# First mixture part: z's two norms on GpSimd, an expert's rounding and low half in its own step

## The chip, the core and the metric

The program runs on one core of a Trainium2 chip. Its engines are TensorE (PE; its weight loads are listed apart as PEld), VectorE (DVE), ScalarE (ACT), GpSimd (POOL) and SyncE (SP), which issues the DMAs. Each engine works through its own list of instructions in order and meets the others only at semaphores. The metric is the time of one execution in microseconds (us).

## The reference, cut to what matters

```python
x = x + 0.5 * ffn(layernorm(x))     # mixture of 8 experts, the best 2 of each row, and a shared expert
x = x + attn(layernorm(x))          # 16 heads, then an MLP; each projection normalises its input again
x = x + 0.5 * ffn(layernorm(x))     # the same mixture once more

def ffn(x):
    scores = sigmoid(x @ gate_W) * route_scale
    topk_scores, topk_idx = top_k(scores, 2)
    gate_full = einsum(topk_scores / topk_scores.sum(-1), one_hot(topk_idx, 8))
    h = gelu(einsum('bsd,edh->bseh', x, W1) + b1)
    expert_out = einsum('bse,bsed->bsd', gate_full, einsum(h, W2) + b2)
    return expert_out + gelu(x @ Ws1 + bs1) @ Ws2 + bs2
```

x is 4096 rows of 256. What the attention reads is z = layernorm(x1) of the first mixture's result x1, normalised once more (zn = layernorm(z)) and transposed (zT).

## The kernel before

It runs four parts one after the other: the first mixture (tiles named f_...), attention (a_...), the MLP (m_...), the second mixture (g_...). The change is in the first mixture alone (`ffn_phase` with `tail` set). The second mixture runs the same function without `tail`: it has no z.

A mixture goes over 8 blocks of 512 rows, numbered 0 to 7, and each block over 9 steps, e = 0 to 8: step 0 is the shared expert, the others are the eight experts. Each float32 operand of a product is split in a rounded high half and a low half, and three products are made of them. For one step the work is:

- TensorE: the first layer fl(e), 6 matmuls of 512 columns into f_hid (L938), and then the second layer of two steps before, sl(e-2), 12 matmuls of 256 columns into f_acc (L980).
- ScalarE: the gelu of f_hid into f_act_out (L515), and hi, the rounding of a hidden tile into the high half of f_hp (L507).
- VectorE: the gating g(e) = gate times f_act_out into f_gated (L737), and lo, the low half of f_hp (L742). Both read two tiles of SBUF. (In blocks 0 and 1 the gate comes from PSUM; from block 2 on from f_gB.)

sl(e) waits for lo(e). What differs between the parts is where hi(e) and lo(e) stand: in the first mixture ScalarE makes hi(e-1) in step e, right after the gelu of e, and VectorE makes lo(e-1) in step e, right after g(e), ahead of the other work of the step. In the second mixture hi(e) stands in step e itself, where it waits for g(e), and lo(e) too: at once in steps 0, 3 and 8, and behind the step's other work in the others.

The other work of VectorE in block i, by step: 1 result(i-1) (L753); 2 the logits of i+1 (L666, L668) and z_stats, the statistics of f_res (L631, L636); 3 choices(i+1), the best two (L685 to L694); 4 gates(i+1), small operations (L701 to L720); 5 zz_stats, the statistics of f_zz; 6 x_stats(i+2) and gate_stack (L727); 7 x_norm(i+2) into f_xn (L652), which waits for GpSimd's x_rstd(i+2); 8 zt_lo (L784); 0 xt_lo (L659).

z of block i-1 goes through three engines during block i: z_stats on VectorE; z_rstds on GpSimd (L589, L590, L592, L602: minus mean, variance + eps, to the power -0.5, their product); z_norm on ScalarE in step 4 (L446, four operations of 128x256, f_zz from f_res); the statistics of f_zz on VectorE in step 5; z_rstds again; zn_norm on ScalarE in step 7 (L446, f_zn from f_zz); the transposes of f_zn on TensorE in step 8 (L905).

GpSimd's list for block i is: expneg(i+1) (L606, a power over 128x32, behind the logits and needed by choices), z_rstds twice, x_rstd(i+2) (L590, L592). The blocks 2 to 5 are two rounds of a loop with two blocks in it; blocks 0, 1, 6 and 7 are written out. Blocks 6 and 7 have no x_stats and no x_norm, block 7 no choices. z of block 7 is normalised inside the attention's first steps, on ScalarE.

Of the kernel before, what the change touches and what calls it, by code (L numbers as in the profile page):

```python
# [23 lines left out]
ALU = mybir.AluOpType  # L24
# [100 lines left out]
def ffn_phase(nc, turns, tag, src, dst, w, tail):  # L125
# [150 lines left out]
    def has(i, ahead=0):  # L276

        return not isinstance(i, int) or 0 <= i + ahead < NB
# [163 lines left out]
    def on_scalar(act):  # L442
# [6 lines left out]
        def z_norm(i):  # L449
            act.wait_ge(s["z_rstd"], i * 2 + 1)  # L450

            act.wait_ge(s["z_out"], i * 16 + 16)
            normalise(zz, res, zrs, zshift, s["z"])

# [54 lines left out]
        def body(i, par, first, last):  # L509
            for e in range(NE):  # L510
                act.wait_ge(s["hid"], i * NE + e + 1)
                if e >= 3 or not first:
# [3 lines left out]
                               bias=b1[:, weights_of(e):weights_of(e) + 1]).then_inc(s["gelu"], 1)  # L516
                if tail or first:
                    if e > 0:
                        hi(i, e - 1, first)
                    elif not first:  # L520
                        hi(i - 1, E, False)
                else:
                    if e == 0 and isinstance(i, int) and i == 1:
                        hi(0, E, False)
                    hi(i, e, first)
                if now("up_x", e, first) and not last:
                    xt_hi(i + 1, 1 - par, up_bank(i))
                if now("gf", e, first) and not last:
                    gate_copy(i + 1)
                if e == 4 and tail and not first:  # L530
                    z_norm(i - 1)
                if e == 7 and tail and not first:
                    zn_norm(i - 1)
                if e == 8 and tail and not first:
# [29 lines left out]
        over_blocks(act, body)  # L564
        if tail:
            hi(NB - 1, E, False)
        return dict(z_norm=lambda: z_norm(NB - 1), zn_norm=lambda: zn_norm(NB - 1),
                    zt_hi=lambda c, ps: zt_hi(NB - 1, c, ps))

    def on_gpsimd(pool):  # L570
# [13 lines left out]
        def rstds(stats, ready, rstd, veps, powed, n, minus_mean=None):  # L584
# [7 lines left out]
            pool.tensor_tensor(rstd[:], rstd[:], mhalf[:], ALU.pow).then_inc(powed, 1)  # L592

        def x_rstd(i):
            rstds(mv, s["stats"], rs, s["veps"], s["rstd"], i + 1)
# [13 lines left out]
        def body(i, par, first, last):  # L609
# [4 lines left out]
            if tail and not first:  # L614
                z_rstds(i - 1, 0)
                z_rstds(i - 1, 1)
            if has(i, 2):
                x_rstd(i + 2)
# [9 lines left out]
    def on_vector(dve):  # L628
# [198 lines left out]
        def body(i, par, first, last):  # L827
            for e in range(NE):
# [4 lines left out]
                if e == 1 and not first:  # L833

                    result(i - 1)
                behind = not (tail or first) and e not in (0, 3, NE - 1)
                if tail or first:
                    if e > 0 and not (tail and first and e == 1):
# [53 lines left out]
        over_blocks(dve, body)  # L892
        if tail:
            lo(NB - 1, E)
        result(NB - 1)
# [1389 lines left out]
```

## Time and profile before

| | us |
|---|---|
| median of 3 runs (2415.49 to 2415.98) | 2415.65 |
| the profiled execution | 2414.72 |
| its span in the profile | 2412.9 |
| first mixture, first layer of block 1 to the attention's first product (53.28 to 275.72) | 222.44 |
| the same stretch, TensorE busy | 215.90 |

The profile is of one execution. A line of the timeline is: start in us, duration in us, engine, line of the kernel, operation, tile written <- tiles read, shape, count, and in square brackets how long the engine had been idle before it and who released it. Neighbouring operations on one engine overlap by some 0.08 us, so that a row's end is a little behind the next row's start. The clock that TensorE was granted is 1.00 in every block of the stretch.

### The profile page before, as it was taken

What the parts mean: (1) busy time and instruction counts of PE and PEld (TensorE: products, weight loads), DVE (VectorE), ACT (ScalarE), POOL (GpSimd) and SP (SyncE); (2) the same over time, 40 slices, a digit from 0 to 9 for tenths busy, and PEclk for the clock granted to TensorE, in tenths of its full rate; (3) what the DMA queues carried; (4) which work ended last, traced back from release to release, by engine and by line L of the source; (5) the groups of instructions that cost most, each with busy time, mean ns of one, the idle gap of its engine ahead of it and who ended that gap; (6) DMA issues with size and microseconds to landing.
All of it is one profiled execution on the core that took longest, in us unless ns stands there. A gap on an engine that the chain in (4) does not pass through costs nothing.

```text
span 2412.9 us, 46345 instructions
## 1 busy us (share of the span) xinstructions
PE 2374.6 (98%) x14512; PEld 2068.2 (86%) x14512; DVE 1867.4 (77%) x3615; ACT 1684.6 (70%) x2932; POOL 1521.8 (63%) x1536
## 2 busy tenths in 40 slices
PE   8999999999999999999999999999999999999999
PEld 7888878888888888888888888888888889998898
DVE  7887687888878788887878878788887875466775
ACT  4555677877878787787878778787787865443444
POOL 1333368787777877778787777878777765542220
PEclk9999999999999999999999999999999999999999
DMA  4744631222212232221223312122221345431332
GB/s 181 264 165 156 211 114 45 96 80 78 96 44 87 61 96 75 64 96 44 87 62 97 102 36 96 44 87 84 82 96 44 110 165 166 137 116 58 130 125 95
DMA packets 131970, 245.67 MB, mean 102 GB/s; under 512 B 7290, under 2 KB 90132, under 8 KB 120052
## 3 DMA queue, kind: packets, MB, share of 16 engines
q1 hardware_dynamic: 131828, 244.15, 31.0%
q8 instruction: 44, 0.72, 0.1%
q14 instruction: 98, 0.80, 0.1%
HBM read 140.12 MB, written 53.67 MB: 80 GB/s over the span
## 4 chain that ended last, share of the span: by engine, by line
PE 83%; DVE 7%; issue 4%; POOL 3%; ACT 2%; DMA 2%; SPq 0%; DVEq 0%; POOLq 0%; ACTq 0%
PE a_ov L1727 20%; PE a_sc L1691 19%; PE a_tr L1703 19%; PE a_pj L1638 7%; PE a_pj L1645 4%; PE g_acc L980 3%; PE g_hid L938 3%; PE f_acc L980 2%; PE f_hid L938 2%; PE m_proj L2141 1%; POOL m_zin L1987 1%; PE m_hid L2210 1%; DMA f_xin<-in_x 1%; DVE f_hp L742 1%; DVE f_gated L737 1%
## 5 line engine op out<-in xcount | busy, mean ns | idle before, releaser
L1594 DVE TENSOR_REDUCE a_nmax<-a_sc 128x1 f32<-128x1024 f32 x512 | 626.8, 1224 | 252.1 <-PE a_sc L1691 248.3
L1437 ACT ACTIVATE a_pT<-a_tr 128x512 fp32r<-128x512 f32 x1024 | 559.6, 596 | 317.2 <-PE a_tr L1703 312.3
L1521 POOL TENSOR_SCALAR a_pr<-a_pr,a_rden 128x1024 f32<-128x1024 f32 x512 | 576.5, 1127 | 282.3 <-DVE a_rden L1599 212.1
L1605 DVE TENSOR_TENSOR a_pT<-a_tr,a_pT 128x512 fp32r<-128x512 f32 x1024 | 650.4, 677 | 17.1 <-ACT a_pT L1437 17.1
L1727 PE MATMUL a_ov<-a_pT,a_v_s 128*128 128x512 f32 x2032 | 594.1, 414 | 1.2 <-DVE f_zT L784 0.8
L1443 ACT ACTIVATE a_pr<-a_sc,a_nmax 128x1024 f32<-128x1024 f32 x512 | 573.7, 1121 | 20.2 <-DVE a_nmax L1594 17.9
L1691 PE MATMUL a_sc<-a_k_s,a_q_s 128*128 128x512 f32 x2048 | 556.6, 393 | 0.6 <-DMA a_k_s<-a_k_s 0.6
L1703 PEld LDWEIGHTS a_tr<-f_ident,a_pr 128*128 128x128 f32 x4096 | 476.0, 140 | 79.8 <-DVE a_pT L1605 7.3
L1703 PE MATMUL a_tr<-f_ident,a_pr 128*128 128x128 f32 x4096 | 537.1, 273 | 1.8 <-DVE a_pT L1605 1.7
L1691 PEld LDWEIGHTS a_sc<-a_k_s,a_q_s 128*128 128x128 f32 x2048 | 376.6, 188 | 76.7 <-DMA a_k_s<-a_k_s 0.8
L1727 PEld LDWEIGHTS a_ov<-a_pT,a_v_s 128*128 128x128 f32 x2032 | 343.8, 189 | 47.5 <-issue 4.8
L1638 PE MATMUL a_pj<-a_z_s,a_wqk_s 128*128 128x512 f32 x756 | 213.9, 392 | 1.5 <-ACT a_staged L1398 1.1
L1638 PEld LDWEIGHTS a_pj<-a_z_s,a_wqk_s 128*128 128x128 f32 x756 | 141.6, 188 | 33.7 <-ACT a_staged L1398 1.4
L980 PEld LDWEIGHTS f_acc<-f_w2p,f_hp 128*128 128x128 f32 x864 | 110.8, 190 | 19.5 <-DVE f_hp L742 14.6
L980 PE MATMUL f_acc<-f_w2p,f_hp 128*128 128x256 f32 x864 | 117.2, 285 | 7.4 <-DVE f_hp L742 7.1
L980 PEld LDWEIGHTS g_acc<-g_w2p,g_hp 128*128 128x128 f32 x864 | 111.9, 191 | 11.3 <-DVE g_hp L742 6.8
L980 PE MATMUL g_acc<-g_w2p,g_hp 128*128 128x256 f32 x864 | 115.7, 284 | 3.4 <-DVE g_hp L742 3.2
L1645 PEld LDWEIGHTS a_pj<-a_wv_s,a_z_s 128*128 128x128 f32 x756 | 105.8, 188 | 12.1 <-issue 0.7
L938 PE MATMUL f_hid<-f_xT,f_w1p 128*128 128x512 f32 x432 | 113.7, 398 | 0.0
L938 PE MATMUL g_hid<-g_xT,g_w1p 128*128 128x512 f32 x432 | 113.0, 397 | 0.0
L515 ACT ACTIVATE f_act_out<-f_hid,f_b 128x512 f32<-128x512 f32 x72 | 49.1, 684 | 91.0 <-PE f_hid L938 91.0
L1645 PE MATMUL a_pj<-a_wv_s,a_z_s 128*128 128x256 f32 x756 | 109.0, 280 | 0.3 <-ACT a_q_s L1405 0.3
(265 smaller groups left out, 3182.0 us busy)
## 6 DMA issues: line engine op xcount, KB each, us to landing
a_z_s<-zT SPq DMA_DIRECT2D x32, 1024.0 KB, 7.8
a_k_s<-a_k_s SPq DMA_DIRECT2D x62, 512.0 KB, 5.6
a_wqk_s<-w_split SPq DMA_DIRECT2D x64, 256.0 KB, 3.1
a_v_s<-a_v_b SPq DMA_DIRECT2D x16, 1024.0 KB, 4.6
att<-a_ao SPq DMA_DIRECT2D x32, 512.0 KB, 2.9
m_in<-att SPq DMA_DIRECT2D x16, 1024.0 KB, 5.9
f_gB<-f_gate_rows SPq DMA_DIRECT2D x12, 1024.0 KB, 4.9
g_gB<-g_gate_rows SPq DMA_DIRECT2D x12, 1024.0 KB, 4.7
```

What stands on the lines that cost most here:

```text
L938: o = pe.matmul(hid[:, (par + e) % 2], w1p[:, a, (c * NE + x) * HID:(c * NE + x + 1) * HID], xT[:, par, c, b], start=(n == 0), stop=(n == 5))
L980: o = pe.matmul(acc[:, t], hp[:, e % 3, a, t * P:(t + 1) * P], w2p[:, b, x * D:(x + 1) * D], start=False, stop=(e == NE - 1 and (a, b) == ...
L1437: act.activation(pT[:, (u // 4) % 2, 0, 4 * part:4 * part + 4, (u % 4) * P:(u % 4 + 1) * P], tr[:, part].rearrange("p (t q) -> p t q", t=4 ...
L1443: act.activation(pr[:, k % NP], sc[:, k % 2], ACT.Exp, bias=nmax[:, k % NP:k % NP + 1], accum_out=den[:, k % NP:k % NP + 1]).then_inc(s["e ...
L1521: pool.tensor_scalar(pr[:, k % NP], pr[:, k % NP], rden[:, k % NP:k % NP + 1], 1.0, ALU.mult, ALU.mult).then_inc(s["normed"], 1)
L1594: dve.tensor_reduce(nmax[:, k % NP:k % NP + 1], sc[:, k % 2], AX.X, ALU.max, negate=True).then_inc(s["negmax"], 1)
L1605: dve.tensor_tensor(to[:, 1], tr[:, part].rearrange("p (t q) -> p t q", t=4), to[:, 0].bitcast(F32), ALU.subtract).then_inc(s["tr_lo"], 1)
L1638: o = pe.matmul(bank[:], wqk_s[:, "QK".index(kind), h, a], z_s[:, h * 2 + b, part], start=(h == 0 and i == 0), stop=(h == 1 and i == 2), s ...
L1645: o = pe.matmul(bank[:, h * 2 * P:(h + 1) * 2 * P], z_s[:, c * 2 + a, part // 2, col:col + P], wv_s[:, c, b], start=(i == 0), stop=(i == 5))
L1691: o = pe.matmul(sc[:, k % 2, kb * BT:(kb + 1) * BT], q_s[:, slot, head, tile * P:(tile + 1) * P], k_s[:, slot, head, a, kb * BT:(kb + 1) * ...
L1703: o = pe.transpose(tr[:, part, j * P:(j + 1) * P], pr[:, (k - LAG) % NP, (4 * part + j) * P:(4 * part + j + 1) * P], ident[:])
L1727: o = pe.matmul(values_bank(v, last)[:], v_s[:, vslot, kt, 2 * vhead:2 * vhead + 2] .rearrange("p k f -> p (k f)"), pT[:, blk % 2, a, kt], ...
```

## The change

GpSimd gets a `normalise` of its own, a `tensor_scalar` with multiply and add and the two per-row numbers as operands, four of 128x256. z_norm and zn_norm of blocks 0 to 6 leave ScalarE's steps 4 and 7 for GpSimd's list: the first right behind the first z_rstds, the second right behind the second, ahead of x_rstd(i+2). z of block 7 stays on ScalarE. In blocks 1 to 7 of the first mixture, hi and lo stand in the expert's own step, as in the second mixture.

```diff
@@ on_scalar
-                if tail or first:
+                if first:
                     if e > 0:
                         hi(i, e - 1, first)
...
-                if e == 4 and tail and not first:
-                    z_norm(i - 1)
-                if e == 7 and tail and not first:
-                    zn_norm(i - 1)
...
-        if tail:
-            hi(NB - 1, E, False)
@@ on_gpsimd
+        def normalise(to, x, ready, n, counted):
+            pool.wait_ge(ready, n)
+            stand_alone(pool, turns)
+            for t in range(NT):
+                o = pool.tensor_scalar(to[:, t], x[:, t], zrs[:, t:t + 1], zshift[:, t:t + 1], ALU.mult, ALU.add)
+            o.then_inc(counted, 1)
...
             if tail and not first:
                 z_rstds(i - 1, 0)
+                pool.wait_ge(s["z_out"], i * 16)
+                normalise(zz, res, s["z_rstd"], i * 2 - 1, s["z"])
                 z_rstds(i - 1, 1)
+                if not (isinstance(i, int) and i == 1):
+                    pool.wait_ge(s["zT_ps"], i * DC - DC)
+                normalise(zn, zz, s["z_rstd"], i * 2, s["zn"])
             if has(i, 2):
                 x_rstd(i + 2)
@@ on_vector
-                behind = not (tail or first) and e not in (0, 3, NE - 1)
-                if tail or first:
+                behind = not first and e not in (0, 3, NE - 1)
+                if first:
...
-        if tail:
-            lo(NB - 1, E)
```

GpSimd in a block of the loop, from the second z_rstds on. Before:

```order
L589 TENSOR_SCALAR f_zshift<-f_zmv 128x4
L590 TENSOR_SCALAR f_zrs<-f_zmv 128x4
L592 TENSOR_TENSOR f_zrs<-f_zrs,f_mhalf 128x4
L602 TENSOR_TENSOR f_zshift<-f_zshift,f_zrs 128x4
L586 REGISTER_ALU
L590 TENSOR_SCALAR f_rs<-f_mv 128x4
L592 TENSOR_TENSOR f_rs<-f_rs,f_mhalf 128x4
```

and now (the line numbers of the changed kernel differ a little; L593 is its normalise):

```order
L584 TENSOR_SCALAR f_zshift<-f_zmv 128x4
L585 TENSOR_SCALAR f_zrs<-f_zmv 128x4
L587 TENSOR_TENSOR f_zrs<-f_zrs,f_mhalf 128x4
L604 TENSOR_TENSOR f_zshift<-f_zshift,f_zrs 128x4
L622 REGISTER_ALU
L593 TENSOR_SCALAR f_zn<-f_zz,f_zrs,f_zshift 128x256 x4
L581 REGISTER_ALU
L585 TENSOR_SCALAR f_rs<-f_mv 128x4
L587 TENSOR_TENSOR f_rs<-f_rs,f_mhalf 128x4
```

Four operations of 128x256 now stand between the second z_rstds and x_rstd (f_rs).

VectorE in a block of the loop, from gate_stack in step 6 to x_norm in step 7 and the gating of step 8. Before:

```order
L727 CAST f_gst<-f_gbc 128x512
L730 REGISTER_ALU
L737 TENSOR_TENSOR f_gated<-f_gB,f_act_out 128x512
L742 TENSOR_TENSOR f_hp<-f_gated,f_hp 128x512
L650 REGISTER_ALU
L652 TENSOR_SCALAR f_xn<-f_xin,f_mv,f_rs 128x256 x4
L730 REGISTER_ALU
L737 TENSOR_TENSOR f_gated<-f_gB,f_act_out 128x512
```

and now:

```order
L734 CAST f_gst<-f_gbc 128x512
L749 TENSOR_TENSOR f_hp<-f_gated,f_hp 128x512
L737 REGISTER_ALU
L744 TENSOR_TENSOR f_gated<-f_gB,f_act_out 128x512
L657 REGISTER_ALU
L659 TENSOR_SCALAR f_xn<-f_xin,f_mv,f_rs 128x256 x4
L749 TENSOR_TENSOR f_hp<-f_gated,f_hp 128x512
L737 REGISTER_ALU
L744 TENSOR_TENSOR f_gated<-f_gB,f_act_out 128x512
```

lo(6) has moved ahead of g(7), and lo(7) from behind g(8) to between x_norm and g(8).

## Rows read from the trace of the kernel before

**Rows 1.** Page, part 1: TensorE's busy us, share of the span, instructions

```profile
PE 2374.6 (98%) x14512; PEld 2068.2 (86%) x14512; DVE 1867.4 (77%) x3615; ACT 1684.6 (70%) x2932; POOL 1521.8 (63%) x1536
```

**Rows 2.** Waits of TensorE, 0 to 282 us: total, times, longest

```profile
PE f_acc L980 <- DVE f_hp L742: 7.1, 16, 1.0
```

**Rows 3.** Windows of blocks 3, 6, 7: length, busy time by engine

```profile
core 0: us, PE busy (x) PEld busy (x) DVE busy (x) ACT busy (x) POOL busy (x), PEclk, DMA share, GB/s
...
117.87:149.51 31.64, 30.59 (x205) 27.24 (x204) 25.45 (x86) 17.34 (x32) 11.50 (x11) 1.00 0.49 168
212.38:242.96 30.58, 30.22 (x205) 27.34 (x204) 23.03 (x74) 17.33 (x32) 9.87 (x9) 1.00 0.47 156
242.96:275.72 32.76, 31.13 (x202) 27.38 (x201) 24.66 (x46) 23.58 (x37) 6.63 (x8) 1.00 0.76 273
```

**Rows 4.** Timeline of TensorE, block 3: start, duration, what, idle before

```profile
137.10 1.70 PE L980 MATMUL f_acc<-f_w2p,f_hp 128*128 128x256 f32 x12 [0.39 <-DVE f_hp L742]
140.54 1.69 PE L980 MATMUL f_acc<-f_w2p,f_hp 128*128 128x256 f32 x12 [0.35 <-DVE f_hp L742]
147.19 1.69 PE L980 MATMUL f_acc<-f_w2p,f_hp 128*128 128x256 f32 x12 [0.32 <-DVE f_hp L742]
150.98 1.60 PE L980 MATMUL f_acc<-f_w2p,f_hp 128*128 128x256 f32 x12
```

**Rows 5.** Timeline of VectorE, block 3

```profile
131.83 0.69 DVE L737 TENSOR_TENSOR f_gated<-f_gB,f_act_out 128x512 f32<-128x512 f32 x1 [0.15 <-ACT f_act_out L515]
135.76 0.69 DVE L737 TENSOR_TENSOR f_gated<-f_gB,f_act_out 128x512 f32<-128x512 f32 x1 [0.55 <-DVE f_idx L694]
145.85 0.68 DVE L737 TENSOR_TENSOR f_gated<-f_gB,f_act_out 128x512 f32<-128x512 f32 x1
146.45 0.69 DVE L742 TENSOR_TENSOR f_hp<-f_gated,f_hp 128x512 fp32r<-128x512 f32 x1
147.56 1.38 DVE L652 TENSOR_SCALAR f_xn<-f_xin,f_mv,f_rs 128x256 f32<-128x256 f32 x4 [0.42 <-POOL f_rs L592]
```

**Rows 6.** Timeline of GpSimd and ScalarE, block 3

```profile
142.53 0.44 POOL L589 TENSOR_SCALAR f_zshift<-f_zmv 128x4 f32<-128x4 f32 x1 [7.66 <-DVE f_zmv L636]
144.80 0.20 POOL L602 TENSOR_TENSOR f_zshift<-f_zshift,f_zrs 128x4 f32<-128x4 f32 x1
145.20 2.06 ACT L446 ACTIVATE f_zn<-f_zz,f_zshift,f_zrs 128x256 f32<-128x256 f32 x4
145.87 1.56 POOL L592 TENSOR_TENSOR f_rs<-f_rs,f_mhalf 128x4 f32<-128x4 f32 x1
```

**Rows 7.** Groups: count, busy us, mean ns; last, L592's min/median/max ns

```profile
L1474 POOL TENSOR_SCALAR a_v_b<-a_staged 128x256 fp32r<-128x256 f32 x64 | 25.9, 405 | 0.0
L2022 POOL TENSOR_SCALAR m_w_in<-m_w_in,m_ln 128x512 f32<-128x512 f32 x2 | 1.4, 728 | 0.0
L507 ACT ACTIVATE f_hp<-f_gated 128x512 fp32r<-128x512 f32 x64 | 39.8, 622 | 0.0
...
L592 POOL TENSOR_TENSOR f_rs<-f_rs,f_mhalf x8: 1037/1562/1589, 7.2 to 208.7; 128x4 f32<-128x4 f32 x8
```

**Rows 8.** Timelines, VectorE beside GpSimd; last, L1569's min/median/max ns

```profile
69.04 0.68 DVE L742 TENSOR_TENSOR f_hp<-f_gated,f_hp 128x512 fp32r<-128x512 f32 x1
69.08 0.78 POOL L590 TENSOR_SCALAR f_zrs<-f_zmv 128x4 f32<-128x4 f32 x1
...
2142.05 3.28 POOL L1987 TENSOR_TENSOR m_xin<-m_xin,m_b 128x256 f32<-128x256 f32 x4 [2.02 <-DMA m_xin<-x]
2143.79 0.95 DVE L2076 TENSOR_TENSOR m_hid_s<-m_act_out,m_hid_s 128x512 fp32r<-128x512 f32 x1 [0.80 <-ACT m_hid_s L1941]
...
L1569 DVE TENSOR_TENSOR a_q_s<-a_staged,a_q_s x4: 684/687/1003, 282.6 to 285.0; 64x512 fp32r<-64x512 f32 x4
```

**Rows 9.** Timeline of TensorE, end of block 7

```profile
270.58 1.06 PE L905 MATMUL f_aux<-f_ident,f_zn 128*128 128x128 f32 x8 [0.15 <-ACT f_zn L446]
272.39 3.49 PE L980 MATMUL f_acc<-f_w2p,f_hp 128*128 128x256 f32 x24 [0.75 <-DVE f_hp L742]
```

More of the change, by code:

```diff
@@ L452, in z_norm @@
             act.wait_ge(s["z_out"], i * 16 + 16)
+            act.wait_ge(s["zn"], i)
             normalise(zz, res, zrs, zshift, s["z"])
```

## The prediction

> **What bounds the kernel now.** I read the page's busy shares first: TensorE is busy 98% of the span [rows 1], so the change can only give back waits of TensorE, or make new ones. Next its waits up to 282 us: second layers (L980) wait 7.1 us for VectorE's low halves, 16 times [rows 2]. The windows say where: block 3 takes 31.64 us, block 6, which has one such wait and no x_stats and x_norm, 30.58 [rows 3]. Block 3 has three, of 0.39, 0.35 and 0.32 us [rows 4]. Two waits more for 1.06 us more: one costs about 0.53, a third of it in matmuls that restart without a preloaded weight. So a steady block (2 to 5) can win at most 3 x 0.53 = 1.6 us, and with blocks 1, 6 and 7 the whole change at most some 10 us.
>
> Who makes the three waits? VectorE from g(3) at 131.83 to the end of lo(6), 146.45 + 0.69 = 147.14, when sl(6) starts at 147.19 [rows 4, 5]. In these 15.3 us it has almost no idle time (the 0.55 behind the choice of the best two is the largest [rows 5]). The low halves are late because they stand behind choices, gates, zz_stats and x_stats: VectorE's work in steps 3 to 6 is long, not ScalarE's. Before step 3 and in steps 8 to 2 it waits for others and catches up. A second chain lies beside it: VectorE's zz_stats, GpSimd's second z_rstds (142.53 to 145.00), x_rstd (its power ends at 145.87 + 1.56 = 147.43), x_norm on VectorE at 147.56, which had already waited 0.42 us for it [rows 5, 6]. What hangs on x_norm is free now: sl(7) starts at 150.98 with no wait [rows 4].
>
> **The change part by part, in a block of the loop.**
>
> 1. *ScalarE is relieved.* Two norms of four operations at 0.52 us (2.06 / 4 [rows 6]) go away, 4.1 us a block. ScalarE is busy 17.3 us of 31.64 [rows 3], and nobody waits for it in steps 3 to 7. Worth 0.
>
> 2. *lo in its own step.* From g(3) to lo(6) the new order has two VectorE operations fewer, lo(2) (now ahead of g(3)) and g(7) (now behind lo(6)). One takes 0.60 us to the next one's start (145.85 to 146.45 [rows 5]): -1.20. In step 3 lo follows its gating at once, so VectorE stands still while ScalarE rounds: 0.62 [rows 7] and some 0.1 of handovers, +0.75. The other roundings of the chain hide behind the step's other work (1.4 us and more). Sum -0.45 us a block in blocks 2 to 6: -2.2.
>
> 3. *The norms on GpSimd, their price.* No row has this form. Bounds: 0.41 us for 128x256 with constant operands (L1474) and 0.73 for 128x512 with one per-row operand (L2022) [rows 7]. I take 0.47, nearer to the row of the same size; four are 1.9 us, which is no more than ScalarE's 2.06. So f_zz comes no later than before, and zz_stats, which stands two steps' work behind it, is not delayed: choices and gates hide the first norm.
>
> 4. *The two engines hold each other up.* In the trace, a GpSimd operation of 128x4 that starts beside L742 takes 0.78 us, where another of 128x4 takes 0.20 [rows 6, 8]: it waits until L742 is through. The other way round: L2076, a subtraction of two SBUF tiles as L742 is, takes 0.95 us inside GpSimd's L1987 instead of 0.68, and L1569 took 1.00 once instead of 0.69 [rows 8]. So a gating or a low half that meets a running norm waits for the rest of one of its four operations, 0 to 0.47 us, and the norm then waits for VectorE's whole pair. On the chain to lo(6) two meetings are likely, one near g(4), one at lo(6), which moved forward to just where the second norm runs: +0.3 us a block in blocks 2 to 6, +1.5. (The Trainium skill, SBUF — State Buffer, section "Who interferes with whom", has the rule behind it: a VectorE instruction with two SBUF inputs contends with a GpSimd instruction that reads SBUF, and the one that comes second is blocked for the whole of the other. By that rule the trace agrees; if it did not hold, this item would be 0 and item 5 smaller.)
>
> 5. *x_rstd stands behind the second norm.* This is the term that decides. z_rstds ends at 145.00 [rows 6]. The second norm takes 1.9 us, held up by the pair lo(6), g(7) for 1.2, with handovers until 148.2. Then x_rstd, 1.4 to 1.5 us (some 0.3 us by my estimate for the sum with eps, and 1.04, the least of L592 [rows 7], for the power, since VectorE now stands still and does not disturb it): x_norm can start at 149.8 instead of 147.56. It takes 1.32, and lo(7), now behind it, 0.68: done at 151.8. sl(7), at 150.98 before and at about 150.8 by items 2 and 4, waits 1.0 us. Without item 4's blocking x_rstd would end 1.2 earlier and lo(7) at about 150.6, just in time: 0 to 1.0, and I take 0.95, since the meeting is nearly certain. Blocks 2 to 5: +3.8.
>
> 6. *What comes after lo(7).* g(8), then lo(8) at once behind its rounding (0.75), zt_lo, lo(0), xt_lo, for which the logits on TensorE wait: with lo(7) late and sl(7) started by it, five operations of 0.60 and two waits stand against two second layers, two first layers and the transposes. The sum is within 0.3 us of even; +0.25 in blocks 2 to 5: +1.0.
>
> 7. *The ends.* Block 1 has its gates in PSUM, so g does not meet the norm; x_norm did not wait there. +0.2. At the end of block 7 TensorE waits 0.15 us for zn and 0.75 for the last low half [rows 9], which both come earlier now: -0.8. What a longer first mixture costs later is nothing: attention takes over where it ends.
>
> Sum: -2.2 + 1.5 + 3.8 + 1.0 + 0.2 - 0.8 = +3.5 us. The profiled execution took 2414.72 us, so 2418.2; the median of the runs lies 0.93 above it, so 2419.2 for the median, +0.15%.
>
> **The rivals.**
>
> - *Slower by more, the norms are dear.* The price of one is up to 0.6 us (the 128x512 of L2022 less its longer row, plus a second per-row operand), and VectorE's small operations of gates, which also read two tiles, meet the first norm: each of four norm operations can hold VectorE once, up to 2 us on the chain to lo(6). Then a steady block loses 1 to 1.5 us more than in my sum: +8 to +13 us, 2424 to 2429. It decides from 0.55 us an operation on. For it: the bound row is an estimate's distance away. Against: in the first norm's time VectorE mostly does the choices, whose search reads little.
> - *Hidden.* The blocking is rare or short, x_rstd comes in time. Then item 2 stays (-2.2), item 4 and 6 fall to 0, item 5 to 0 or +1, the end gives -0.8: -2 to -3, 2412 to 2414. For it: the two engines met in blocks 2 to 6 before too, and none of the f_gated and f_hp rows of block 3 is longer than 0.69 [rows 5].
> - *The waits go.* The low halves are ready a step earlier for sl(3), whose wait stood behind the choices, and the 0.55 us of idle time behind the search [rows 5] goes with the order; with no blocking the block drops towards block 6's 30.58 [rows 3]: 5 x 1.0 + 0.8, so -5 to -9, 2407 to 2411. Against: the sum of VectorE's work to lo(6) hardly shrinks.
> - *Nothing moves*: gains and waits cancel, or VectorE's chain stays as it is; within the bound of no change.
>
> **How the numbers follow.** My sum with its own spread, 0 to +8 us (item 5 between 0.5 and 1.5, item 4 between 0.1 and 0.6): 0.50. Dear norms: 0.15. Hidden: 0.20. The waits go: 0.13. Nothing moves: 0.02. A measurement of this kernel tells 0.2% from no change, 4.8 us: 2410.8 to 2420.5 counts as the same. Of my own case 0.30 lies within and 0.20 above. Faster 0.13, same 0.52 (0.30 + 0.20 + 0.02), slower 0.35 (0.20 + 0.15). The range leaves out the upper end of dear norms and most of the last gain: 2412 to 2427.
>
> **What the changed profile would show.** GpSimd's norm rows: 0.45 to 0.5 us each when undisturbed, with some of 1 us and more in which VectorE's pair ran. x_norm (f_xn) with an idle time of 1.5 to 2.5 us before it, released by GpSimd, instead of 0.42. TensorE with a new wait at the first second layer of a block, sl(7), of about 1 us, and perhaps a small one at the logits; the waits at sl(3) gone, at sl(4) and sl(6) still there. f_gated and f_hp rows over 0.8 us in steps 4 and 6 to 7. ScalarE idle before each rounding, as in the second mixture. No f_gated or f_hp row longer than 0.7 would show item 4 wrong; x_norm at its old distance from zz_stats would show item 5 wrong; and if item 5 is wrong, so is the sign of the whole.

## The result, and the profile after

The changed kernel takes 2429.60 us in the median of four runs (2429.05 to 2432.94), the kernel before 2415.57 (2415.01 to 2415.98): a ratio of 1.0058, with a 95% interval of 1.0046 to 1.0070. That is 14 us slower. The sign that the sum gave is right, the size is not: 2419.2 was predicted, with 2427 as the upper end.

Nearly all of the loss lies in the first mixture: its blocks 1 to 7 take 13.9 us more, and the spans of the two profiled executions differ by 14.3 (2427.2 and 2412.9). The windows of the changed kernel by block, 1 to 7, each from one first layer of step 0 to the next; the columns are those of [rows 3]:

```profile
53.01:85.41 32.40, 31.95 (x214) 28.97 (x212) 26.67 (x85) 13.00 (x21) 15.02 (x19) 1.00 0.43 151
85.41:121.35 35.94, 32.42 (x205) 28.86 (x204) 27.84 (x90) 14.14 (x24) 15.92 (x19) 0.95 0.79 305
121.35:152.73 31.38, 30.55 (x206) 27.36 (x204) 23.33 (x78) 13.92 (x23) 16.01 (x19) 1.00 0.44 161
152.73:185.49 32.76, 31.08 (x205) 27.33 (x203) 25.55 (x84) 13.88 (x23) 16.28 (x20) 1.00 0.45 160
185.49:219.98 34.49, 32.58 (x206) 28.69 (x204) 25.75 (x84) 13.87 (x23) 16.37 (x20) 0.95 0.43 149
219.98:255.39 35.41, 32.60 (x206) 28.62 (x204) 25.98 (x79) 14.65 (x25) 16.47 (x18) 0.95 0.41 148
255.39:289.39 34.00, 30.18 (x201) 27.33 (x200) 24.36 (x45) 19.60 (x28) 14.67 (x16) 1.00 0.75 260
```

The third column from the right is the granted clock. It was 1.00 in every block before; now it is 0.95 in blocks 2, 5 and 6. Against the same windows of the kernel before:

| block | before, us | after, us | difference | made up of |
|---|---|---|---|---|
| 1 | 32.54 | 32.40 | -0.1 | |
| 2 | 32.05 | 35.94 | +3.9 | late transfer of f_xin 2.2, clock 1.7 |
| 3 | 31.64 | 31.38 | -0.3 | no wait at its first second layer, block 2 being late |
| 4 | 31.45 | 32.76 | +1.3 | waits |
| 5 | 31.42 | 34.49 | +3.1 | waits 1.4, clock 1.7 |
| 6 | 30.58 | 35.41 | +4.8 | waits 3.1 (1.05 at sl(7), 0.35 at the logits, 1.6 for f_zn), clock 1.7 |
| 7 | 32.76 | 34.00 | +1.2 | waits for f_zz and f_zn |
| sum | 222.44 | 236.38 | +13.9 | clock 5.1, transfer 2.2, the rest waits |

A fall of the clock is priced from two blocks of one kernel with nearly the same waits: block 5 less block 4 here is 34.49 - 32.76 = 1.7 us, and three pairs in the experiments give 1.7 to 1.8 as well. Where a block had a fall, the column gives it 1.7 us and the wait the rest; that is a way to share out the difference and not a measurement of each part.

**A steady block without the clock.** TensorE in block 4, the rows that answer to [rows 4]:

```profile
155.25 1.70 PE L985 MATMUL f_acc<-f_w2p,f_hp 128*128 128x256 f32 x12 [0.88 <-DVE f_hp L749]
...
159.04 1.60 PE L985 MATMUL f_acc<-f_w2p,f_hp 128*128 128x256 f32 x12
160.72 1.95 PE L920 MATMUL f_gbc<-f_gwp,f_xT 128*128 128x16 f32 x16
...
182.81 1.70 PE L985 MATMUL f_acc<-f_w2p,f_hp 128*128 128x256 f32 x12 [0.30 <-DVE f_hp L749]
```

The wait at sl(3) is gone, those at sl(4) (0.25 us, not shown) and sl(6) stay, and sl(7) at 155.25 waits 0.88 us. The logits at 160.72 start 1.68 us behind the start of sl(8) where 1.44 is normal, and take 1.95 instead of 1.85: the row has no wait in brackets, but against the usual start they are 0.24 us late.

The cause of the late sl(7) is on GpSimd and VectorE (the first group of rows is GpSimd's, the second VectorE's); they answer to [rows 5, 6]:

```profile
181.42 3.10 POOL L593 TENSOR_SCALAR f_zn<-f_zz,f_zrs,f_zshift 128x256 f32<-128x256 f32 x4 [0.21 <-POOL f_zshift L604]
...
184.81 1.04 POOL L587 TENSOR_TENSOR f_rs<-f_rs,f_mhalf 128x4 f32<-128x4 f32 x1
```

```profile
182.07 0.69 DVE L749 TENSOR_TENSOR f_hp<-f_gated,f_hp 128x512 fp32r<-128x512 f32 x1
182.68 0.88 DVE L744 TENSOR_TENSOR f_gated<-f_gB,f_act_out 128x512 f32<-128x512 f32 x1
...
185.98 1.38 DVE L659 TENSOR_SCALAR f_xn<-f_xin,f_mv,f_rs 128x256 f32<-128x256 f32 x4 [2.42 <-POOL f_rs L587]
187.27 0.69 DVE L749 TENSOR_TENSOR f_hp<-f_gated,f_hp 128x512 fp32r<-128x512 f32 x1
```

x_norm had waited 0.42 us for f_rs; now 2.42. Behind it stands lo(7) at 187.27, for which sl(7) at 188.02 had waited 0.90.

**What one norm costs.** All 28 operations of each of the two norms (duration in ns: least, median, largest):

```profile
L593 POOL TENSOR_SCALAR f_zz<-f_res,f_zrs,f_zshift x28: 548/556/2549, 70.8 to 275.5; 128x256 f32<-128x256 f32 x28
L593 POOL TENSOR_SCALAR f_zn<-f_zz,f_zrs,f_zshift x28: 549/556/1590, 81.3 to 284.5; 128x256 f32<-128x256 f32 x28
```

0.556 us, not 0.47. (The Trainium skill, GPSIMD Engine Reference, section "Elementwise — side-by-side cycle accounting", gives 2.6 cycles an element for an operation with two tensor inputs; an estimate from it, at the page's 1.2 GHz, is 0.555 us for 256 elements. The trace has that number, 0.556, for an operation with one tensor input and two per-row operands, a form which the section does not name. The section "Engine selection" of the same page calls one-input operations roughly line-rate, and for this form, one input and two per-row operands at 0.556 us, the trace disagrees.)

**The clock.** Two windows of 2 us behind block 5's logits, same columns (in the ones before and behind them the clock is 1.00), and TensorE's rows there:

```profile
196.00:198.00 2.00, 2.00 (x8) 1.66 (x8) 0.16 (x1) 0.48 (x1) 1.76 (x1) 0.54 0.41 80
198.00:200.00 2.00, 2.00 (x13) 2.00 (x13) 1.77 (x5) 0.84 (x2) 2.00 (x1) 0.61 1.08 380
```

```profile
193.49 1.95 PE L920 MATMUL f_gbc<-f_gwp,f_xT 128*128 128x16 f32 x16
195.29 2.19 PE L943 MATMUL f_hid<-f_xT,f_w1p 128*128 128x512 f32 x6
197.28 1.05 PE L977 MATMUL f_acc<-f_b2s,f_gst 128*128 128x256 f32 x4
```

From about 196 to 199.5 the granted clock was 0.50, the lower of the two levels (1.2 instead of 2.4 GHz), while TensorE was busy all the time: six products of 512 columns took 2.19 us instead of 1.63, and the four of L977 1.05 instead of 0.64. Nothing is marked as waiting in these rows. A reader who counts waits alone misses 1.7 us.

**Block 2.** SP's rows of before, then of after. The first is two loads of gates into f_gB with a wait between them, the second the first store of the split weights, the last the load of f_xin:

```profile
81.12 4.57 SPq L375 DMA_DIRECT2D f_gB<-f_gate_rows  x2
85.73 0.43 SPq L326 DMA_DIRECT2D w_kept<-f_w1p  x1
...
95.59 7.62 SPq L403 DMA_DIRECT2D f_xin<-in_x  x1
```

```profile
82.73 5.43 SPq L375 DMA_DIRECT2D f_gB<-f_gate_rows  x2
88.21 0.43 SPq L326 DMA_DIRECT2D w_kept<-f_w1p  x1
...
96.05 9.67 SPq L403 DMA_DIRECT2D f_xin<-in_x  x1
```

VectorE at the end of block 1, g(8) in before, then x_norm and g(8) in after:

```profile
84.64 0.69 DVE L737 TENSOR_TENSOR f_gated<-f_gbc,f_act_out 128x512 f32<-128x512 f32 x1
```

```profile
85.23 1.38 DVE L659 TENSOR_SCALAR f_xn<-f_xin,f_mv,f_rs 128x256 f32<-128x256 f32 x4 [1.73 <-POOL f_rs L587]
...
87.13 0.68 DVE L744 TENSOR_TENSOR f_gated<-f_gbc,f_act_out 128x512 f32<-128x512 f32 x1
```

and, in after, x_stats on VectorE and sl(6) on TensorE:

```profile
114.31 1.40 DVE L638 BATCH_NORM_STATS2 f_st<-f_xin 128x6 f32<-128x256 f32 x4 [2.49 <-DMA f_xin<-in_x]
```

```profile
117.48 2.81 PE L985 MATMUL f_acc<-f_w2p,f_hp 128*128 128x256 f32 x12 [2.88 <-DVE f_hp L749]
```

Why the load is late is read from these rows and from the kernel. The second of the two loads into f_gB waits for the semaphore `gated`, that is for g(8) of block 1 (`sp.wait_ge(s["gated"], used)`), and the 5 MB of split weights stand behind it in SP's list. g(8) starts at 87.13 instead of 84.64: x_norm of block 1 waits 1.73 us for f_rs, where it waited for nothing before, and lo(7), 0.60, now stands ahead of g(8). So the stores start 2.5 us later, at 88.21. In each of the eight kernels in which x_stats waits for this load, it ends that wait 25.6 to 26.1 us behind the start of the stores: 111.77 in before, 114.31 here. It is item 5 of the prediction once more, x_rstd behind the second norm, in a block where TensorE does not feel it and SP does. The copy of the gates to f_gf is 1.6 us late too (80.65 instead of 79.03, behind the rounding of step 6), but it has time: in norms_only (below) it is on time, g(8) starts at 86.87, and the load lands at 113.83 all the same. x_stats waits only 0.73 us for it there, since it comes later itself.

### The profile page after: what moved, and what is told of

The parts are those of the page before. It is cut to its first block, busy times and chain, and to the rows that moved or that the text cites. A ratio compares the mean times of both kernels' runs of the same rounds, so it can differ in the third digit from the quotient of the medians.

```text
span 2427.2 us, 46362 instructions
## 1 busy us (share of the span) xinstructions
PE 2381.7 (98%) x14512; PEld 2074.7 (85%) x14512; DVE 1869.1 (77%) x3615; ACT 1662.8 (69%) x2876; POOL 1556.3 (64%) x1592
## 4 chain that ended last, share of the span: by engine, by line
PE 78%; DVE 3%; issue 3%; POOL 2%; ACT 1%; DMA 1%; DVEq 0%; SPq 0%; POOLq 0%; ACTq 0%
PE a_ov L1732 19%; PE a_sc L1696 19%; PE a_tr L1708 18%; PE a_pj L1643 7%; PE a_pj L1650 4%; PE g_acc L985 3%; PE g_hid L943 3%; PE m_proj L2146 1%; POOL m_zin L1992 1%; PE m_hid L2215 1%; PE m_acc L2186 0%; POOL m_xin L1992 0%; PE g_gbc L920 0%; DMA m_xin<-x 0%; DVE g_gated L744 0%
## 5 line engine op out<-in xcount | busy, mean ns | idle before, releaser
L508 ACT ACTIVATE f_hp<-f_gated 128x512 fp32r<-128x512 f32 x64 | 40.4, 631 | 94.8 <-DVE f_gated L744 94.8
```

## The experiments

Thirteen kernels; a steady block is block 4 where nothing else is said (31.45 us before, 32.76 after). The ratio behind each time is that to the kernel before, with its 95% interval.

**own_step_only and norms_only: each half alone.**

```diff
 own_step_only, against the kernel before
-                if tail or first:        # ScalarE: hi(e - 1) in step e
+                if first:
-                behind = not (tail or first) and e not in (0, 3, NE - 1)
+                behind = not first and e not in (0, 3, NE - 1)
 norms_only: the changed kernel with these lines as before
```

> The kernel before with hi and lo in the expert's own step; both norms stay on ScalarE. Theory A (the norms on GpSimd are the whole cost, by holding x_norm and the transposes of f_zn up, and TensorE's lower clock follows from those waits): nothing late at sl(7), x_stats of block 2 waits for its DMA at most 0.5 us, clock 1.00 in every block; by items 2 and 7 of the prediction 2411 to 2416 us, at most 2416. Theory B (the order of hi and lo is the cost, since VectorE stands still for each rounding in step 3 and ScalarE's work is late): 2422 us or more, with the waits at sl(4), sl(6) and the clock drops kept. If the late gate row of block 1 comes from the order and not from the norms, block 2 alone keeps a wait for f_xin of some 2 us here (+2 to +4).

> The changed kernel with hi and lo back at the places of before (hi(e-1) and lo(e-1) in step e); both norms stay on GpSimd. Theory A: most of the loss stays, since x_rstd still stands behind the second norm and f_zn is still late in blocks 6 and 7: 2424 to 2432 us, a wait of TensorE for f_zn in blocks 6 and 7. lo(6) is a step later here, so the second norm meets other work: the wait at the second layer moves to sl(6) or sl(7) and is 0.5 to 1.5 us. Theory B: the loss goes with the order: 2414 to 2418 us.

Measured: own_step_only 2426.87 us, 1.0047 (1.0030 to 1.0064); norms_only 2425.44 us, 1.0040 (1.0026 to 1.0054). Both theories fall: either half alone costs 10 to 12 us, and both together not 22 but 14. No block of either has a granted clock under 1.00. The steady block of each, own_step_only first:

```profile
155.20:188.43 33.23, 30.79 (x205) 27.27 (x204) 25.81 (x85) 18.02 (x31) 11.12 (x11) 1.00 0.44 158
```

```profile
153.18:186.73 33.55, 30.88 (x206) 27.18 (x204) 26.17 (x84) 13.63 (x24) 17.19 (x19) 1.00 0.45 157
```

33.2 and 33.6 us: each is worse in a steady block than the whole change (32.8). In own_step_only the cause is a new wait, once in each of blocks 1 to 7; ScalarE's two rows show why:

```profile
187.61 1.07 PE L901 MATMUL f_aux<-f_ident,f_zn 128*128 128x128 f32 x8 [1.64 <-ACT f_zn L446]
```

```profile
184.86 0.63 ACT L507 ACTIVATE f_hp<-f_gated 128x512 fp32r<-128x512 f32 x1 [1.67 <-DVE f_gated L735]
185.40 2.07 ACT L446 ACTIVATE f_zn<-f_zz,f_zshift,f_zrs 128x256 f32<-128x256 f32 x4
```

hi(7), now in its own step, waits for g(7) and holds zn_norm behind it. So the two halves of the change need each other: the own step makes ScalarE a bad place for the norm where it stands. In norms_only x_norm waits 2.42 us as in the whole change, and lo(6) and lo(7) stand a step later, so that sl(7) waits 1.05, sl(4) 0.94 and sl(6) 0.53.

**x_first: x_rstd(i+2) ahead of the second norm.**

```diff
                 z_rstds(i - 1, 1)
+                if has(i, 2):
+                    x_rstd(i + 2)
...
                 normalise(zn, zz, s["z_rstd"], i * 2, s["zn"])
-            if has(i, 2):
-                x_rstd(i + 2)
```

> The changed kernel with x_rstd(i+2) ahead of the second norm in GpSimd's list. Item 5 of the prediction (x_rstd behind the norm makes x_norm, lo(7) and sl(7) late): the wait of x_norm for f_rs falls from 2.4 us to 0.5, the 0.9 us at sl(7) go in blocks 2 to 5, which is worth 3 to 4 us, and with them two of the three clock drops (another 3 us): 2422 to 2425 us. Against it: f_zn comes some 1.5 us later, and its transposes in step 8, which wait 0.16 to 0.24 us in blocks 2 to 5 now, wait 1 us and more there; if that is the tighter place, the wait only moves and the time is 2428 to 2432.

Measured: 2425.13 us, 1.0039 (1.0024 to 1.0053). The wait at sl(7) is gone and another stands a step ahead of it; the first row is the transposes of f_zn, the second sl(7), 1.47 us behind its first layer, without a wait, and the last the logits, which are in time:

```profile
153.98 1.07 PE L912 MATMUL f_aux<-f_ident,f_zn 128*128 128x128 f32 x8 [1.56 <-POOL f_zn L593]
...
156.27 1.60 PE L987 MATMUL f_acc<-f_w2p,f_hp 128*128 128x256 f32 x12
...
161.40 1.84 PE L922 MATMUL f_gbc<-f_gwp,f_xT 128*128 128x16 f32 x16
```

Its steady block, 32.7 us, is that of the changed kernel. GpSimd has the second norm and x_rstd to do between z_rstds and the end of the block, 4.5 us of work (3.10 and 1.35), and something waits for whichever is second. The time came out near the range expected, but not for the reason expected: a steady block won nothing. Blocks 5 and 6, in which the clock now stays at 1.00, take 1.8 and 3.3 us less than in the changed kernel; block 1 takes 2.7 us more (35.06), with a wait of 2.1 us for f_zn and a fall of the clock behind it, and block 7 1.3 more, with a fall too.

**keep_late and keep_early: the 5 MB of split weights elsewhere in SP's list.**

```diff
         body(1, 1)
-        if tail:
-            keep_weights()
 keep_late: behind body(NB - 2, 0) and store_qkv(2); keep_early: behind body(0, 0)
```

> The changed kernel with the three stores of the split weights (2304, 512 and 2304 KB) behind block 6 in SP's list, not behind block 1. Theory C (block 2's 3.9 us are a transfer: the stores start 2.5 us later and the load of f_xin lands late among them, x_stats waits 2.5 us, TensorE waits 2.9 us and its clock drops): block 2 falls from 35.94 to 31.8 to 32.4 us, no drop there, 2425 to 2427 us; blocks 5 and 6 keep theirs, unless the stores meet block 6. If the wait of x_stats was GpSimd's and not the transfer's, block 2 stays at 35 us and more and the time at 2429.

> The changed kernel with the three stores of the split weights ahead of the first store_qkv, behind block 0 in SP's list. With the stores behind block 6 the wait of x_stats for f_xin in block 2 went, but the time was lost at the start of attention, where TensorE waited 8.3 us for zT behind them. Theory C: block 2's wait of 2.9 us at sl(6) goes and nothing new comes if block 1 has room for 5 MB: 2426 to 2428 us. If the stores are in the way in block 1 instead (its gate rows and f_xres, or the load of f_xin for block 3), the wait moves there and the time is 2429 to 2433.

Measured: keep_late 2440.44 us, 1.0102 (1.0086 to 1.0119), of which a wait of 8.3 us for zT at the start of attention, behind the stores; keep_early 2431.63 us, 1.0071 (1.0054 to 1.0088). In both, x_stats of block 2 waits for no transfer and sl(6) only 0.32 us, so that part of theory C holds. But block 2 fell only to 33.9 us in both, since the waits of a steady block and a fall of the clock came in their place, and in blocks 3 to 6 the clock fell three times in each instead of twice. The whole time did not show what the edit cured, the block did. Net, little was to be had here: blocks 2 and 3 of keep_early take 65.0 us together without their two falls, at 1.7 each, those of the changed kernel 65.6 without its one, since block 2's lateness had spared block 3 its wait at sl(7). Where no such wait follows, in best (below), the transfer's absence is worth 1.4 us.

**warm: work for TensorE in the wait at sl(7).**

```diff
+                if tail and e == 0 and (par == 1 and not isinstance(i, int) or isinstance(i, int) and i == NB - 2):
+                    pe.wait_ge(s["gst"], i + 1)
+                    pe.wait_ge(s["gf"], i - 1)
+                    for t in range(6):
+                        pe.transpose(gbc[:, t % 2, 0:P], ident[:], ident[:])
                 if e >= 2:
...
                     second_layer(i - 1, E - 1 + e, 1 - par, False)
```

> The changed kernel with six transposes of the identity into an unused place of f_gbc on TensorE ahead of sl(7) in the first step of blocks 3, 5 and 6. They add work to the 0.9 us in which TensorE waits there for lo(7), and take no wait away. Theory D (the lower clock of blocks 5 and 6 follows from that idle time a few us earlier): no granted clock under 0.95 near 196 and 230 us, the two blocks shorter by 1.6 us each, 2426 to 2427 us. Rival: the clock falls for another reason (all the waits together, or the small matmuls of the logits), the two drops stay, 2429 to 2431 us.

Measured: 2429.32 us, 1.0060 (1.0043 to 1.0076), as the changed kernel. The transposes stand in blocks 3, 5 and 6. In block 6 the idle time at sl(7) fell from 0.90 to 0.23 us, and the clock fell all the same, at 232 us; it fell in block 3 too, which had no wait there. In block 5 it stayed, but so it did in block 5 of keep_early, with a wait of 0.88. Theory D has this against it. Nor does it explain norms_only, where sl(7) waits 1.05 us and the clock stays:

```profile
155.86 1.70 PE L989 MATMUL f_acc<-f_w2p,f_hp 128*128 128x256 f32 x12 [1.05 <-DVE f_hp L751]
...
161.08 1.85 PE L924 MATMUL f_gbc<-f_gwp,f_xT 128*128 128x16 f32 x16
```

What it has and the changed kernel lacks is logits that start at once: 161.08 is 1.42 us behind the start of sl(8). This led to theory F: late logits, and not the wait at sl(7), bring the lower clock.

**xt_first and late_logits: the logits in time in one kernel, late in the other.**

```diff
 xt_first, against the changed kernel, step 0 of blocks 1 to 6
+                        xt_hi(i + 1, 1 - par, up_bank(i))      # ScalarE
                     hi(i, e, first)
+                        xt_lo(i + 1, 1 - par, up_bank(i))      # VectorE
                         lo(i, e)
 late_logits, against the kernel before
+                            for t in range(NT):
+                                o = dve.bn_stats(st6[:, t], w2p[:, 0, t * 352:(t + 1) * 352].bitcast(F32))
+                            o.then_inc(s["late"], 1)
+                            dve.wait_ge(s["late"], i)
                         xt_lo(i + 1, 1 - par, up_bank(i))
```

> The changed kernel with the high and low halves of f_xT ahead of hi(0) and lo(0) in step 0 of blocks 1 to 6. Seen so far: the clock fell only 2.5 to 3.7 us behind logits that had themselves waited 0.24 us for the low half of f_xT (in the changed kernel, keep_late, keep_early and warm, though not behind each of them), and never behind logits that did not wait, also not in norms_only, whose sl(7) waits 1.05 us shortly before. Theory F (the late logits, not the wait at sl(7), bring the lower clock): the waits of 0.9 us at sl(7) stay, the logits start 1.43 us behind the start of sl(8), the drops of blocks 5 and 6 go; 2 x 1.6 us and 4 to 5 x 0.35: 2424 to 2426 us. Rival (theory D, the wait at sl(7) brings it): drops stay, 2427 to 2429.

> The kernel before with four statistics more on VectorE (of 128x352 each, of a constant tile, into a scratch tile, unused) ahead of the low half of f_xT in step 0 of blocks 1 to 6, so that the logits wait 0.2 to 0.4 us and nothing else on TensorE does. Theory F: two to five of the six blocks show a granted clock of 0.50 for some 3.4 us a few us behind the logits, at 1.6 us each, and with 6 x 0.35 for the waits 2420 to 2426 us. Theory D: no drop, since nothing waits at sl(7); only the waits are paid: 2416.5 to 2418 us.

Measured: xt_first 2426.01 us, 1.0039 (1.0024 to 1.0054); late_logits 2423.36 us, 1.0030 (1.0018 to 1.0041). Block 5 of xt_first and TensorE in it; then blocks 3 and 5 of late_logits, and TensorE in block 3 (the logits start 1.68 us behind sl(8)):

```profile
186.41:219.03 32.62, 30.80 (x206) 27.27 (x203) 25.74 (x84) 13.76 (x23) 16.79 (x20) 1.00 0.46 169
```

```profile
188.93 1.70 PE L989 MATMUL f_acc<-f_w2p,f_hp 128*128 128x256 f32 x12 [0.89 <-DVE f_hp L751]
...
194.16 1.84 PE L924 MATMUL f_gbc<-f_gwp,f_xT 128*128 128x16 f32 x16
```

```profile
122.17:155.66 33.49, 32.44 (x205) 28.63 (x203) 27.08 (x90) 17.33 (x32) 11.63 (x11) 0.95 0.47 159
...
188.99:220.72 31.73, 30.90 (x205) 27.33 (x204) 27.03 (x90) 17.34 (x32) 11.53 (x11) 1.00 0.47 166
```

```profile
129.02 1.95 PE L920 MATMUL f_gbc<-f_gwp,f_xT 128*128 128x16 f32 x16
```

In xt_first the wait of 0.89 us at sl(7) stays and the clock stays at 1.00 in blocks 4 to 6. In late_logits no second layer waits over 0.02 us longer than before, only the logits do, and the clock falls in blocks 1, 3 and 4; blocks 3 and 4 take 1.8 and 1.6 us more than block 5. Theory F holds both ways. Over the profiles of all 15 kernels the logits of blocks 1 to 6 were late 34 times (0.1 to 0.4 us behind their usual start, once 1.2) and the clock fell within some us behind 22 of them; 56 times they were in time, and it fell behind none. Which of the late ones bring it down stays open: neighbouring blocks with the same rows differ.

**zn_ahead and zz_pool: the second norm on ScalarE, ahead of hi(7).**

```diff
 both, on ScalarE
+                    if e == 7 and tail:
+                        zn_norm(i - 1)
                     hi(i, e, first)
 zn_ahead: the first norm on ScalarE too; zz_pool: the first norm on GpSimd
```

> The kernel with only the order of hi and lo changed (both norms on ScalarE, 2426.9 us), and zn_norm ahead of hi(7) in step 7. There the transposes of f_zn waited 1.64 us a block, since hi(7), which waits for g(7), stood ahead of the norm. Theory E (that place alone is why the order without the GpSimd norms costs 12 us): the wait falls to 0 to 0.4 us, a steady block from 33.2 to 31.4 to 31.9, 2415 to 2418 us. Rival (ScalarE is too full for this order: gelu(5) behind z_norm makes sl(6) late, and hi(7) behind zn_norm makes lo(7) late): a wait at sl(7) takes its place, 2422 to 2426.

> The changed kernel with the second norm back on ScalarE, in step 7 ahead of hi(7); the first norm stays on GpSimd. Item 3 of the prediction (the first norm is hidden) and item 5 (the second is not) together: x_norm waits 0.4 us again, no wait at sl(7), no clock drop in blocks 5 and 6, sl(4) 0.3 and sl(6) 0.3 stay: a steady block 31.1 to 31.5 us, 2413 to 2417 us with block 2's transfer solved, 2417 to 2419 with it. If the first norm's mutual blocking with VectorE costs on the chain to lo(6), the block stays at 32 and the time at 2420 to 2424.

Measured: zn_ahead 2418.55 us, 1.0015 (1.0006 to 1.0025); zz_pool 2414.16 us, 0.9999 (0.9989 to 1.0009). The steady block of each, zn_ahead first:

```profile
152.12:183.53 31.41, 30.63 (x205) 27.29 (x204) 25.63 (x86) 17.79 (x31) 11.11 (x11) 1.00 0.48 168
```

```profile
150.35:181.28 30.93, 30.38 (x206) 27.37 (x203) 25.52 (x86) 15.82 (x27) 13.73 (x15) 1.00 0.47 164
```

31.4 and 30.9, against 31.45 of before. So theory E holds: the place of one norm is why own_step_only lost. The second norm on GpSimd costs 32.76 - 30.93 = 1.8 us a block, waits alone; the first norm there saves 0.5, since on ScalarE it delays gelu(5) and with it lo(6) (sl(6) waits 0.53 us there, 0.30 in zz_pool). zz_pool still loses 2 us in block 2 (34.02, the transfer and one fall of the clock behind the 1.85 us at sl(6)) and 1.2 in block 7 (33.96).

**best, best_lo6 and mixed: towards a faster kernel.**

```diff
 best: zz_pool, keep_weights() behind body(0, 0), and in block 7
-                behind = not first and e not in (0, 3, NE - 1)
+                behind = not first and not (tail and last) and e not in (0, 3, NE - 1)
 best_lo6: best, and lo(6) at once too:  e not in (0, 3, 6, NE - 1)
 mixed: zz_pool, keep_weights() behind body(0, 0), block 7 in all as in the kernel before
```

> zz_pool (the first norm on GpSimd, the second on ScalarE ahead of hi(7)) with the stores of the split weights behind block 0 and, in block 7, lo at once in each step. In zz_pool the steady block takes 30.9 us against 31.45 of before, and the rest is lost in block 2 (34.0 us, x_stats waits 1.45 us for f_xin, TensorE 1.85, one clock drop) and in block 7 (33.96, sl(5) waits 1.3 us for a low half behind zz_stats). Theory: block 2 goes to 30.9 to 31.3, block 7 to 32.7 to 33.2, block 1 costs 0.6 more as in keep_early: 2410 to 2412.5 us, 0.1 to 0.2% under before. Rival (the stores cost in block 1 or before it what they spare, the wait in block 7 is made by zz and moves to the next step): 2413 to 2415.

> best, with lo(6) at once behind its rounding, ahead of x_stats and the gate stack. The wait at sl(6), 0.3 us idle and 0.46 from start to start in each block, is the largest left in a steady block. If x_norm and lo(7), some 0.6 us later by this, still come in time for sl(7): 0.45 us a block less, 2408 to 2410. If they don't, sl(7) and the logits wait: 0 to 1 us a block more and drops of the clock, 2411 to 2420.

> best, with block 7 of the first mixture as in the kernel before: hi(e-1) and lo(e-1) in step e, both norms on ScalarE in steps 4 and 7. In best, block 7 took 34.70 us against 32.76 of before, with a wait of 1.77 us for f_zn and 0.78 at sl(6), while the five blocks ahead of it took 30.5 to 30.9 against 30.6 to 32.0. If the loss of block 7 is of the norm on GpSimd beside the long VectorE operations of 128x1024 and of the order there: block 7 takes 32.6 to 33.0, the others stay, 2411.5 to 2413.5 us, 0.1 to 0.2% under before. Rival (block 7 is late because it starts earlier and meets a transfer or the attention's loads): block 7 stays at 34 and more, 2414 us.

Measured: best 2414.26 us, 0.9991 (0.9982 to 1.0001); best_lo6 2426.19 us, 1.0041 (1.0026 to 1.0056); mixed 2413.27 us, 0.9989 (0.9980 to 0.9998). Block 2 of best, block 7 of best, block 7 of mixed:

```profile
86.08:117.01 30.93, 30.36 (x206) 27.36 (x204) 25.32 (x85) 15.84 (x27) 13.76 (x15) 1.00 0.49 170
...
240.22:274.92 34.70, 31.41 (x202) 27.27 (x200) 25.84 (x47) 21.97 (x34) 9.91 (x12) 1.00 0.81 280
```

```profile
242.11:274.93 32.82, 31.18 (x202) 27.42 (x201) 25.02 (x47) 23.70 (x38) 6.62 (x8) 1.00 0.80 293
```

Block 2 falls from 34.02 to 30.93, so the transfer and the fall of the clock behind it are worth 3.1 us (1.4 and 1.7). The new order in block 7 does not work: it lost there in best and is back at before's 32.8 in mixed. One reason is in view in best: GpSimd's product of 128x4, which takes 0.20 us elsewhere, takes 1.15 beside a VectorE operation of 128x1024, and the norm 4.19:

```profile
256.12 1.15 POOL L605 TENSOR_TENSOR f_zshift<-f_zshift,f_zrs 128x4 f32<-128x4 f32 x1
257.58 4.19 POOL L594 TENSOR_SCALAR f_zz<-f_res,f_zrs,f_zshift 128x256 f32<-128x256 f32 x4 [0.31 <-POOL f_zshift L605]
```

```profile
255.93 1.28 DVE L780 SCALAR_TENSOR_TENSOR f_qkv_in<-f_qkv_in,f_ln 128x1024 f32<-128x1024 f32 x1
```

In best_lo6 the wait at sl(6) went; 0.9 us at sl(7), late logits and four falls of the clock took its place, 11.9 us more than best for an edit meant to save 2. mixed is faster than the kernel before by 0.11%, which is less than the 0.2% that the prediction called measurable; its interval barely leaves out no change. The early stores have a price of their own, late logits in block 1 of best and mixed, and in the profile of mixed a fall of the clock there. The medians of best and zz_pool are not to be compared with each other, since the kernel before took 2415.95 us beside best and 2414.70 beside zz_pool. Against it best is 1.7 us faster and zz_pool 0.5; that difference of 1.2 is close to the 1.7 us by which attention's first product starts earlier in best (274.92 against 276.61), but less than the intervals can tell.

## Why the prediction was wrong, point by point

The steps that failed are three. The clock of TensorE was put at no change without a reason: 5.1 us. The late x_norm was priced for sl(7) alone, and not in block 1, where it delays SP's stores and with them the load for block 2: 2.2 us. And the ends were put at a gain of 0.8 us, where blocks 6 and 7 wait for f_zn and f_zz: 1.6 and 1.2 us lost.

- **Item 1, ScalarE relieved, 0.** Wrong. The cover that hid z_norm, "nobody waits for ScalarE in steps 3 to 7", was read from the old order. In the own step it is no longer true: with the first norm on ScalarE (zn_ahead) a steady block takes 0.5 us more than without it (zz_pool), and in own_step_only the second norm, left in its old place, makes TensorE wait 1.6 us a block.
- **Item 2, the own step, -0.45 a block.** Right in size where nothing else is late: zz_pool's steady block is 0.5 us shorter than before. These are the same 0.5 us as in item 1: in zn_ahead the order has won them by sl(4), which starts 21.95 us into the block instead of 22.46, and the norm on ScalarE takes them back at sl(5) and sl(6). Alone, in own_step_only, the edit costs 1.8.
- **Item 3, the price of a norm, 0.47 us.** 0.556; four of them take 2.2 undisturbed instead of 1.9. Each norm also has 0.21 us of idle time ahead of it. The bounds of 0.41 to 0.73 held it. That the first norm is hidden held in blocks 2 to 6 and not in block 7, where its four operations took 5.5 us and the statistics of f_zz waited 1.4.
- **Item 4, mutual blocking, +0.3 on the chain to lo(6).** The blocking is there: the second norm takes 3.10 us where lo(6) and g(7) run, and g(7) takes 0.88. But on the chain to lo(6) no cost shows: sl(6) waits 0.30 us, as before. All of it falls on the norm, and so on item 5. (The Trainium skill's rule of "SBUF — State Buffer", section "Who interferes with whom", that the later one is blocked for the whole of the other, agrees with the 1.15 us of a 128x4 product beside L780 as well.)
- **Item 5, x_rstd behind the second norm, 0.95 us at sl(7).** Right at sl(7): 0.88 to 0.90, three times, 1.05 from start to start. x_norm's wait of 1.5 to 2.5 us was 2.42. Three of the four came (behind blocks 3, 4 and 5); behind block 2, which was already late for the transfer, there was none. The other thing that hangs on x_norm, SP's list in block 1, is the last point below.
- **Item 6, the logits, +0.25 a block.** Right as a wait, 0.24 and 0.10 more in the logits themselves. Wrong in what it leads to, and this is **the largest miss**: late logits can bring the clock down, and two such falls in blocks 5 and 6 cost 3.4 us; the third, 1.7, came behind block 2's wait. The clock was 1.00 in every block before, and the prediction took it as given. No rival has it either.
- **Item 7, the ends, -0.6 in sum.** Wrong in sign. Block 7 took 1.2 us more, and block 6 was not priced for f_zn, for which it waits 1.40 us (1.6 from start to start): the norm, between VectorE's pairs, takes 4.09 us there instead of 3.10, and sl(6), without x_stats ahead of lo(6), has no wait that would cover it. This is the same question as item 5, who comes behind a slower norm, and it was asked for one tile of the two. Of block 1 the item says that x_norm did not wait there; now it waits 1.73 us.
- **Not in the sum: block 2's transfer, 2.2 us.** The step that was skipped is what else stands behind a late instruction: g(8) of block 1 stands behind x_norm and lo(7), SP's second load of gates behind g(8), 5 MB of stores behind that, and behind them a load for which x_stats had already waited 0.24 us in the kernel before. keep_late and keep_early show that the stores are the cause; that g(8) starts them is read from the rows and the kernel's text, and no run moved it alone.

Added up for a steady block the prediction gave +1.05 us, and blocks 4 and 5 show +1.3 and +1.4 without the clock. The mechanism in the loop was right, and the waits at sl(7) and the logits in block 6's window, 1.4 us, belong to it. Outside it lay 5.1 us of clock, 2.2 of transfer, 1.6 of block 6's wait for f_zn and 1.2 in block 7. The rival "dear norms" named the time (2424 to 2429) more closely, and its condition, 0.55 us an operation, was met by a hair, but its mechanism, VectorE held on the chain to lo(6), is not what happened.

Of the signs in the profile named beforehand, most came: x_norm's wait, 1 us at sl(7), the late logits, sl(3) without a wait, g(7) over 0.8 us. Two did not: an undisturbed norm row of 0.45 to 0.5 us (it is 0.556), and a long g or lo in step 4 (0.69 and 0.68 in block 4). Those that came show where the sum was sound. The sum left out a cost that no wait shows.

## What to carry to other kernels

An engine whose busy share is 98% at full clock has a second thing to lose beside waits: here logits that started 0.24 us late were followed by falls of the clock that cost 1.7 us each. So read the granted clock in windows of 2 us before adding up waits. When work is moved to another engine or step, list everything that stands behind it and behind whatever it makes late, in every block and not only the steady one, the waits of the engine that issues the transfers included; and when two edits come together, ask of each whether the reason that makes it cheap is still true once the other is in.

## What the runs showed of the hardware

- TensorE's granted clock fell from 1.00 to 0.50 although TensorE had been busy without a gap but for 0.24 us ahead of sixteen products of 16 and 8 columns, some 3 us earlier (block 5 of the changed kernel). A wait of 1.05 us at sl(7) in norms_only, or of 1.64 us ahead of the transposes of f_zn in own_step_only, brought no fall, and six transposes put into the idle time at sl(7) did not prevent one. In the first mixture's blocks 1 to 7, ten of eleven waits of 1.85 to 3.0 us brought one too.
- A fall costs 1.7 us here, in four pairs of blocks of one kernel with nearly the same waits (34.49 and 32.76 in the changed kernel; 33.49 and 31.73 in late_logits; 33.69 and 31.97 in best_lo6; 34.49 and 32.81 in keep_early).
- A tensor_scalar of 128x256 on GpSimd with two per-row operands takes 0.556 us, the median of 28 and of 28 more; ScalarE takes 0.52 for the same work.
- SP's issue of the 512 KB load of f_xin takes 0.39 us where the 5 MB of stores stand elsewhere (keep_late, keep_early), and 5.8 to 9.8 us behind them (7.62 in before, 9.67 in after, 5.80 in x_first, 9.76 in xt_first): the issue itself is held up, and with it all that stands behind it in SP's list. The data of that load is there 25.6 to 26.1 us behind the start of the stores, in eight kernels.
